# One decoder layer on one core: reordered key and query products, first transposes, last expert's copies, and idle transposes near the end

## What is computed

```
x = x + attn_ref(layernorm(x))          # linear attention read from a stored memory M, z; then @ Wo.T
x = x + xattn_ref(layernorm(x), ctx)    # cross attention: 32 query heads, 4 key/value heads of 128,
                                        # keys and values of [ctx, latents]: q = latents@Wq, k, v = hidden@Wk, @Wv,
                                        # softmax(q k^T / sqrt(128)) v, then @ Wo
x = x + ffn_ref(layernorm(x))           # router: softmax over 64 experts, top 8, out = flat*w_sum + w_dense @ expert_bias
```

## Time and profile before

| | us |
|---|---|
| three runs | 699.23, 699.68, 699.2 (median 699.23) |
| the profiled execution | 699.29, of which the span from first to last instruction 697.5 |
| busy in the span | PE 687.2, DVE 520.5, ACT 351.1, POOL 133.8 |
| mean of one 128x512 matmul of line 907 | 0.396 |
| mean of one row-normalising multiply (L2026) | 0.811 |
| chain that ended last | PE 93%, DVE 3%, ACT 2%, POOL 1%, issue 1% |
| mean granted clock of TensorE | 0.996 of full speed |

### The profile page before, as it was taken

One profiled execution on the slowest core, in us unless ns is written; L12 is line 12 of the kernel. 1 busy time (PEld: TensorE's weight loads), 2 busy tenths in 40 slices (PEclk: granted clock), 3 DMA queues, 4 the chain that ended last, 5 costly groups with the idle time before them and its releaser, 6 DMA issues.

```text
span 697.5 us, 11041 instructions
## 1 busy us (share of the span) xinstructions
PE 687.2 (99%) x3560; PEld 579.3 (83%) x3560; DVE 520.5 (75%) x1098; ACT 351.1 (50%) x1047; POOL 133.8 (19%) x136
## 2 busy tenths in 40 slices
PE   8999999999999999999999999999999999999996
PEld 7888888888878788888888888888888888788884
DVE  3774966778877888677678876767877657878887
ACT  4454845455443454454346643555635435755543
POOL 0296000000512232022020220210202000322321
PEclk9999999999999999999999999999999999999998
DMA  9996240001325557433342733423643414231101
GB/s 329 371 351 245 67 145 1 1 0 46 121 76 193 184 160 251 142 122 106 107 152 68 233 105 105 150 84 103 191 143 113 141 41 129 77 115 61 46 32 60
DMA packets 70605, 90.14 MB, mean 129 GB/s; under 512 B 4192, under 2 KB 48480, under 8 KB 70560
## 3 DMA queue, kind: packets, MB, share of 16 engines
q1 hardware_dynamic: 65632, 81.71, 35.7%
q10 hardware_dynamic: 4928, 7.87, 3.1%
HBM read 62.29 MB, written 27.26 MB: 128 GB/s over the span
## 4 chain that ended last, share of the span: by engine, by line
PE 93%; DVE 3%; ACT 2%; POOL 1%; issue 1%; ACTq 0%; DVEq 0%; POOLq 0%
PE bank L978 24%; PE bank L907 23%; PE bank L727 13%; PE bank L1091 8%; PE bank L881 6%; PE bank L1147 6%; PE bank L1121 4%; PE bank L718 2%; PE bank L1047 1%; PE bank L846 1%; PE bank L768 1%; PE bank L812 1%; DVE forms L1566 1%; PE bank L802 1%; PE bank L750 0%
## 5 line engine op out<-in xcount | busy, mean ns | idle before, releaser
L978 PE MATMUL bank<-regA,oT 128*128 128x512 f32 x762 | 180.2, 391 | 0.2 <-DVE oT L1566 0.2
L978 PEld LDWEIGHTS bank<-regA,oT 128*128 128x128 f32 x762 | 142.0, 188 | 29.6 <-DVE oT L1566 0.4
L1474 ACT ACTIVATE probs<-bank,negmax 128x128 f32<-128x128 f32 x256 | 89.9, 377 | 42.8 <-DVE negmax L2007 42.8
L907 PE MATMUL bank<-xnT,forms 128*128 128x512 f32 x432 | 108.8, 396 | 0.5 <-DVE qbuf L1776 0.4
L907 PEld LDWEIGHTS bank<-xnT,forms 128*128 128x128 f32 x432 | 79.0, 188 | 17.6 <-DVE qbuf L1776 1.9
L907 PE MATMUL bank<-regC,forms 128*128 128x512 f32 x324 | 83.8, 397 | 1.6 <-DVE qbuf L1776 0.9
L1181 ACT CAST oT<-bank 128x512 fp32r<-128x512 f32 (+1 forms) x66 | 37.7, 573 | 79.5 <-PE bank L1147 76.5
L907 PEld LDWEIGHTS bank<-regC,forms 128*128 128x128 f32 x324 | 59.0, 188 | 13.4 <-DVE regC L1566 1.3
L1181 ACT CAST pT<-bank 128x512 fp32r<-128x512 f32 x64 | 34.6, 593 | 66.9 <-PE bank L1121 66.7
L727 PE MATMUL bank<-regC,xnT 128*128 128x512 f32 x256 | 68.0, 396 | 0.0
L648 POOL TENSOR_TENSOR diff<-wq_raw 128x256 f32<-128x256 f32 x17 | 13.4, 786 | 283.3 <-DVE forms L1566 283.3
(11 more groups left out here) (195 smaller groups left out, 1058.8 us busy)
## 6 DMA issues: line engine op xcount, KB each, us to landing
q_dram<-qbuf SPq DMA_DIRECT2D x32, 512.0 KB, 3.2
qbuf<-q_dram SPq DMA_DIRECT2D x31, 512.0 KB, 4.8
raw<-in_L_xattn_Wo SPq DMA_DIRECT2D x4, 2048.0 KB, 10.5
wq_raw<-in_L_xattn_Wq SPq DMA_DIRECT2D x16, 512.0 KB, 4.1
raw<-in_L_attn_Wo SPq DMA_DIRECT2D x6, 1024.0 KB, 8.9
k_ring<-keys_dram SPq DMA_DIRECT2D x32, 128.0 KB, 3.5
v_raw<-vals_dram SPq DMA_DIRECT2D x64, 64.0 KB, 3.4
resid<-in_x SPq DMA_DIRECT2D x4, 512.0 KB, 11.6
```

Source lines behind the costliest of these rows:

```text
L907: last = nc.tensor.matmul(k_bank[:, :], forms[:, p[1], a, i, c, :], right(b)[:, c, :], start=j == 0, stop=j == 5)
L978: last = nc.tensor.matmul(bank[7][:, :], oT[:, a, h, :], wo[:, b, h, :], start=h == 0 and i == 0, stop=h == GH - 1 and i == 2)
L1474: last = nc.scalar.activation(probs[:, bb, p, :], bank[bb][:, p * P:(p + 1) * P], ACT.Exp, bias=negmax[:, bb, p:p + 1], accum_out=rowsum[: ...
```

## The change

It has six parts, all in the order of work or in where a small piece of it is done.

1. **First transposes (PE).** One idle transpose instead of three between the transposes of context tiles 0 and 1. Tile 1's first chunks need only the parts that are ready (`early` now for both tiles). The transposes of tiles 2 and 3 come three matmuls earlier.
2. **Latent values and pair 0 (PE, ACT, DVE).** The last latent value product goes to bank 0 instead of 3, so pair 0's second product no longer waits for its copy. ACT makes the token blocks 1 and 2 ahead of that copy. DVE does `sum_11` ahead of `sum_u2` for pair 0.
3. **S2 rounding moved (DVE; ACT for pair 1).** `summed_low` is split: S3 and S1 (`outer_low`) stay ahead of `sum_u3`, S2 (`inner_low`) comes behind `sum_21`, for every pair in the run of seven.
4. **Steps 24 and 25 (DVE, POOL).** DVE rounds head 2 in step 24, and heads 6 and 7 in step 25, ahead of and behind the normalising; POOL has heads 3 to 5.
5. **The last tile's copies (ACT, DVE).** ACT copies the last tile's transposes ahead of scaling the rows of the tile before; DVE takes the negated maximum in one reduction, and the top eight after it.
6. **Twelve idle transposes (PE)** ahead of the wait for the last tile's weights.

```diff
@@ bank of the last latent value product
+            if (kind, i) == ("vlat", NT - 1):
+                return bank[0]
             return bank[2 + i % 2]
...
@@ POOL, low parts of Wo
-            for h in range(4, GH):
+            for h in range(3, GH - 2):
...
@@ PE, start
-            spin(3)
+            spin(1)
             context_transposes(4, (1,))
             for t, c in ((0, 0), (0, 1), (1, 0), (1, 1), (0, 2), (1, 2), (0, 3), (1, 3)):
-                if (t, c) == (0, 3):
+                if (t, c) == (1, 2):
                     context_transposes(1)
-                early = t == 0 and c < 2
+                early = c < 2
...
@@ PE, pairs
             def product_4(p):
-                pe.wait_ge(q_summed, 7 * p[0] + 2)
+                pe.wait_ge(q_summed, 7 * p[0] + 2 if follows(p[0], 1) else 1)
...
             def product_5(p):
+                if not follows(p[0], 1):
+                    pe.wait_ge(q_summed, 2)
...
                 if p == 0:
-                    pe.wait_ge(mm_act, mm_act_count(mm("vlat", 7)))
                     pe.wait_ge(sig_lo, 2 * NT)
...
@@ PE, end
             expert_mix(NT - 2)
+            spin(12)
             expert_weights(NT - 1)
...
@@ ACT, pair 0
-            for t in range(NT):
+            for t in range(NT - 1):
                 save_latent_values(t)
...
                 if t == 6:
-                    summed_high(1, 1)
+                    outer_high(1, 1)
+            act.wait_ge(mm_done, mm("vlat", NT - 1) + 1)
             t_high(1)
+            t_high(2)
+            save_latent_values(NT - 1)
             for p in range(LEAD + 1):
-                if p == 0:
-                    t_high(2)
                 copy_1(p)
                 if p == 0:
                     t_high(3)
+                    inner_high(1, 1)
...
@@ ACT, end
             save_expert_weights(NT - 2)
+            save_last_xn()
             scale_rows(NT - 2)
-            save_last_xn()
...
@@ DVE, pairs
-            summed_low(1, 1)
+            outer_low(1, 1)
             t_low(1)
+            t_low(2)
             for p in range(LEAD + 1):
                 if p:
                     direct_low(p + 1, (p + 1) % 2)
+                if p == 0:
+                    sum_11(p)
                 sum_u2(p)
                 if p == 0:
-                    t_low(2)
-                if p < LEAD:
+                    t_low(3)
+                elif p < LEAD:
                     sum_11(p)
-                if p == 0:
-                    t_low(3)
                 if p < LEAD:
                     if p:
-                        summed_low(p + 1, (p + 1) % 2)
+                        outer_low(p + 1, (p + 1) % 2)
                     sum_u3(p)
                     sum_21(p)
+                    inner_low(p + 1, (p + 1) % 2)
                     sum_22(p)
...
@@ DVE, maximum of the last tile
+                if e == NT - 1:
+                    nc.vector.tensor_reduce(top[:, r, 1, 0:1], logits, axis=AX, op=ALU.max, negate=True)\
+                        .then_inc(e_max_ready, 1)
+                    settled(nc.vector.max(top[:, r, 0, :], logits))
...
@@ DVE, steps 24 and 25
+                if last_group and t == 1:
+                    dve.wait_ge(wo_lo, GH * (KV - 1) + GH - 2)
+                    wo_low(KV - 1, GH - 2)
...
+                if last_group and t == 1:
+                    wo_low(KV - 1, GH - 1)
...
-                    for h in range(2, 4):
+                    for h in range(2, 3 if p is None else 4):
                         wo_low(g, h)
```

More of the change, by code:

```diff
@@ L901, in _ @@
                 pe.wait_ge(tr_used, tr("latent", t) + 1)
+                if t == NT - 1:
+                    pe.wait_ge(tr_used, tr("latent", NT - 2) + 1)
                 values(mm("vlat", t), wkv2, xn_cols, t)
@@ L1081, in step @@
                 if first_step:
+                    pe.wait_ge(mm_act, mm_act_count(mm("vlat", NT - 1)))
                     pe.wait_ge(tr_used, tr("latent", NT - 1) + 1)
@@ L1203, in scale_keys, with outer_high @@
                 act.wait_ge(k_scaled, p + 1)
-            def summed_high(p, slot):
+            def outer_high(p, slot):
                 act.wait_ge(form_summed, 4 * p + 1)
@@ L1209, in summed_high, with inner_high @@
                 high(form_dst(slot, 0, S1), raw_pair(p, 1)).then_inc(form_hi, 1)
+            def inner_high(p, slot):
                 act.wait_ge(form_summed, 4 * p + 4)
                 high(form_dst(slot, 0, S2), raw_pair(p, 0)).then_inc(form_hi, 1)
+            def summed_high(p, slot):
+                outer_high(p, slot)
+                inner_high(p, slot)
             def copy_1(p):
@@ L1765, in direct_low, with outer_low @@
                 low(form_dst(slot, 1, A11), raw_weights(p)[:, :, 0:P], form_dst(slot, 0, A11)).then_inc(form_lo, 1)
-            def summed_low(p, slot):
+            def outer_low(p, slot):
                 dve.wait_ge(form_hi, 4 * p + 2)
@@ L1771, in summed_low, with inner_low @@
                 low(form_dst(slot, 1, S1), raw_weights(p)[:, :, P:2 * P], form_dst(slot, 0, S1)).then_inc(form_lo, 1)
+            def inner_low(p, slot):
                 dve.wait_ge(form_hi, 4 * p + 4)
                 low(form_dst(slot, 1, S2), raw_weights(p)[:, :, 0:P], form_dst(slot, 0, S2)).then_inc(form_lo, 1)
+            def summed_low(p, slot):
+                outer_low(p, slot)
+                inner_low(p, slot)
             def sum_into(dst, left, k_bank):
@@ L1794, in sum_11 @@
                 if not follows(p, 1):
+                    dve.wait_ge(q_copied, 1)
                     dve.wait_ge(t_lo, 2)
@@ L1803, in sum_u3 @@
                 dve.wait_ge(q_done, 7 * p + 4)
-                dve.wait_ge(q_summed, 7 * p + 1)
+                dve.wait_ge(q_summed, 7 * p + 2)
                 sum_into(u3[:, :], u2[:, :], bank[2][:, :])
@@ L1926, in expert_max @@
                                                            in1=rout_b, op0=ALU.mult, op1=ALU.add))
-                settled(nc.vector.max(top[:, r, 0, :], logits))
-                nc.vector.tensor_scalar(top[:, r, 1, 0:1], top[:, r, 0, 0:1], -1.0, None, ALU.mult)\
-                    .then_inc(e_max_ready, 1)
+                if e == NT - 1:
+                    nc.vector.tensor_reduce(top[:, r, 1, 0:1], logits, axis=AX, op=ALU.max, negate=True)\
+                        .then_inc(e_max_ready, 1)
+                    settled(nc.vector.max(top[:, r, 0, :], logits))
+                else:
+                    settled(nc.vector.max(top[:, r, 0, :], logits))
+                    nc.vector.tensor_scalar(top[:, r, 1, 0:1], top[:, r, 0, 0:1], -1.0, None, ALU.mult)\
+                        .then_inc(e_max_ready, 1)
                 nc.vector.match_replace(rest, top[:, r, 0, :], logits, TAKEN).then_inc(e_rest_ready, 1)
```

## The result

| | before | changed |
|---|---|---|
| median of 21 runs each, same chip | 699.38 us | 700.70 us |
| ratio | | 1.0019, 95% interval 1.0012 to 1.0025 |
| span of the profiled execution | 697.5 | 698.4 |
| PE busy | 687.2 | 689.4 |

The forecast was 698.4, in a range of 696.2 to 700.1. The time is outside it, on the side of rival C. As a difference, -0.8 was forecast and +1.3 was measured.

What follows compares the result with a forecast made beforehand. PE was taken as the bound, busy 687.2 of 697.5 us. Start -0.2, pairs -0.7, steps 24 and 25 +0.8 and end -0.7 sum to -0.8: 699.29 becomes 698.5, median 698.4, range 696.2 to 700.1.

Steps and rivals of the forecast that it cites:

- rival C: Pair rounds exceed their parts' sum, with S2 low beside POOL and the store beside the load; +0.4 gives 700.0; chance 0.13.
- Part 1, start: First transposes: fewer idle transposes and earlier first chunks of tile 1 save 0.2 us, bounds 0 and 0.35.
- Part 2, pair 0: Pair 0: PE's waits for ACT's copy and for DVE go, so it ends 2.2 us earlier.
- Part 3, the pairs: Pairs behind pair 0: weight loads pace them instead of PE, leaving only 0.7 us less by the first maximum.
- the sum of the round: One load-to-load round in the pairs: 9.9, or 10.15 with the longer transfer, mean 10.03 us against PE's 9.55.
- Rival A: Pairs: the loads don't pace them, so 3.6 us less there and 695.5 in all; chance 0.13.
- Part 4, steps 24 and 25: Steps 24 and 25: head 6 waiting for POOL and later router weights cost 0.8 us more, bounds -0.5 and +1.0.
- The 0.33 at the second multiply: Step 25: DVE's second normalising multiply, beside POOL's low part of the values, ends 0.33 us later than before.
- the later transfer: Router's weights: loads issued 1.5 us later give PE 0.55 us of new wait.
- Rival B: Steps 24 and 25: none of the new work reaches PE, -0.5 instead of +0.8, so 697.1; chance 0.18.
- Parts 5 and 6, the end: Last tile: earlier copies, one-reduction maximum and a full clock save 0.7 us, limited by ACT's scaling; bounds -0.3 and -1.1.
- Rival D: End: idle transposes don't hold the clock, so the end gives -0.5 to 0 and the time 698.6 to 699.1; chance 0.08.

Runs made afterwards that it cites:

- experiment 1: Changed kernel with S2's low part put back ahead of sum_u3 and sum_21 for pairs 2 and later: 696.63 us.
- experiment 3: Changed kernel with the first half's store of a pair's sums issued behind sum_u4 instead of sum_21: 699.46 us.
- experiment 10: Changed kernel with S2's low part between sum_u3 and sum_21, and the first half's store issued behind sum_u4: 697.68 us.
- experiment 6: Changed kernel with S2's low part between sum_u3 and sum_21 for pairs 2 and later: 699.81 us.
- experiment 11: Changed kernel with DVE's roundings of S3 and S1 waiting for POOL's fourth sum, pairs 2 and later: 705.92 us, a single run.
- experiment 7: Changed kernel with S2's low part ahead of the sums (pairs 2 and later) and heads of steps 24 and 25 shared as before: 696.35 us.
- experiment 5: Changed kernel without the twelve idle transposes ahead of the last tile's weights: 700.67 us.
- experiment 2: Kernel before with S2's low part moved behind sum_21 for pairs 2 and later: 703.49 us.
- experiment 8: Kernel before with only the latent-value and pair 0 change, pair 1's S2 staying behind sum_21: 696.96 us.

## Why the prediction was wrong

**Part 1, start: right.** -0.22 against -0.2, of which -0.12 was left at pair 0.

**Part 2, pair 0: right in mechanism and size.** -2.25 beyond what the start had left, against -2.2; both waits gone, the first load at 208.62 against 208.65.

**Part 3, the pairs: right in the mechanism, wrong in a size, and that decided.** "From here the loads pace the pairs, not PE" held: they did, by `sum_21` and S2, and experiment 1 shows that this order and nothing else did it. The step that failed is the sum of the round: "Sum 9.9, and 10.15 where the transfer takes as long as the last one ... Mean 10.03". It measured 10.58. The terms were read from rows of the kernel before, and the change moved what stood beside them:
- The transfer is the term that was mis-sized: two rows of before, 3.66 and 3.91, gave the two sums (mean 3.79), and in the changed kernel's four rounds it took 4.15 to 4.40, mean 4.27. The load no longer precedes the store of sums by 1.4 but by 0.4. That is 0.48 of the 0.55. In experiments 3 and 10, which move the store alone (against the changed kernel and against 6), all landings are 3.7 to 3.9 again, and the rounds 10.1 to 10.2 but for the one of 11.0 and one of 10.4.
- The other 0.07 is on DVE's S1 rounding, which now meets POOL's fourth sum. The same meeting costs 0.4 on the way to S2's high part, which makes that second chain as long as the first (experiments 6, 11).

The second round of before already showed that meeting, with 10.21 from load to load; the earlier trace rows is the shortest round, where S1's rounding (217.54) began behind POOL's fourth sum:

```profile
226.66 0.99 POOL L656 TENSOR_TENSOR wq_raw<-wq_raw 128x256 f32<-128x256 f32 x1
226.97 2.06 DVE L1566 TENSOR_TENSOR forms<-wq_raw,forms 128x512 fp32r<-128x512 f32 x2
```

Four rounds of 0.55 are 2.2: the last load at 250.95 against 248.8, the first maximum at 256.91 against 254.8. -0.7 became about +1.5. This is rival C: it named the store next to the load in SP's queue, counted 0.4 on a round and had 700.0. It was given 0.13, with "POOL had finished its sums by then" against it. That holds for S2's low part (218.61, POOL done at 217.91) but not for S3's and S1's (215.65 and 216.56), and these are what met POOL.

**Rival A** failed: the loads did pace the changed kernel's pairs. With S2 ahead they do not, but even then most of A's 0.34 a pair does not come: in experiment 7 the first maximum is at 252.96, 2.57 sooner than before, about 2.3 without the start, where A had 3.6. That is pair 0's gain and little more. DVE's roundings ahead of `sum_21` hold the pairs at 9.87.

**Part 4, steps 24 and 25: right in sign, 0.25 instead of 0.8.** Head 6 waited for POOL as forecast (602.97 against 603.1, after taking off the shift of 1.38 that came with the pairs). The 0.33 at the second multiply did not come: POOL's low part of the values took 0.74 instead of 1.17 and the multiply beside it 1.13 instead of 1.48, so the multiply ended at 607.14, or 605.76 less the shift, 0.06 sooner than before. Only the later transfer was left, and the loads went out at 606.4 instead of 606.8 by the same count. Rival B had this way in part (POOL's operations shorter), but its -0.5 did not come either.

**Parts 5 and 6, the end: right.** -0.60 against -0.7, clock 1.00, bound by ACT's scaling. But nearly all of it is ACT's and DVE's order; the clock is worth 0.1, too little for the runs to tell. Rival D's rule, the Trainium skill's page TensorE: Matmul & The Clock Gate, section "Part 4: PE-mode transpose", that transposes don't count as activity in the same way, is not borne out here: with twelve of them the granted clock stayed at 1.00 until the last products were done, in the changed kernel and in all eight experiments that have them. Without them the products ran at a lowered clock in three traces of four (before: 0.59 in 692 to 694; experiment 5: 0.60; experiment 2: 0.54 in 697 to 698), and at the full one in experiment 8.

**The sum.** With 10.58 in place of 10.03 and 0.25 in place of 0.8, the prediction's own count gives 698.4 + 2.2 - 0.55 = 700.1; measured 700.7. In the traces the span grew by 0.9, in the medians the time by 1.3. The difference of 0.4 lies in which execution was profiled: it took 700.22, 0.48 below the median of its 21 runs. What makes the typical run longer than that one isn't settled.

## What to carry to other kernels

Moving a step to behind two others also moves what it releases: here a load, which came to stand directly ahead of a store that had been 1.4 us away. Before adding up a new cycle from old durations, list what will run beside each term in the new order and give the terms that touch a shared resource their loaded value; with four or five rounds an error of half a microsecond on one is more than the whole gain. Where a stage is paced by a cycle of load, rounding and release, put whatever releases the load first.

## What the runs showed of the hardware

- The landing of a 512 KB load (counted from its issue to its first use) took 3.7 to 4.0 us with a store of the sums issued 1.2 us or more behind it, and 4.0 to 4.5 with it 0.4 to 0.6 behind.
- POOL's sum of 128x256 takes 0.74 alone and 1.07 when a DVE rounding with both inputs in SBUF has begun before it; DVE's 128x512 rounding took 0.95 instead of 0.69 when POOL was first.
- Twelve 128x128 transposes, with nothing else on PE, in a gap of some 2 us between products kept the granted clock at 1.00 in all nine traces that have them. With the gap idle the clock fell to 1.2 GHz ahead of or within the last products in three traces (means of 0.59 and 0.60 in two microseconds, 0.54 in one), and only about at their end in the fourth (experiment 8).
